# Score masks moved into the free contraction rows of a two-layer attention kernel, and one output turn per unit instead of two

## Chip, cores and metric

One core of one Trainium2 chip. The metric is the device time of one launch in microseconds, the median of several executions. TensorE is PE in the profile (its weight loads PEld), VectorE DVE, ScalarE ACT, GpSimd POOL, SyncE SP.

## What is computed

Two transformer layers on x of 4 x 1024 x 128, in float32 precision. The parts that the change touches are the two masked attentions of 16 heads of 8:

```
# layer 0, xn = layernorm(x)
scores = einsum('bhqd,bhkd->bhqk', q / sqrt(8), k)
scores = where(pos_q >= pos_k, scores, -inf)
out    = einsum('bhqk,bhkd->bhqd', softmax(scores), v) @ Wout.T
x = x + out + fp4_ffn(xn)                 # blockwise FP4 feed-forward

# layer 1, xn = layernorm(x); keys: the first token, then a convolution of stride 3 (342 keys)
mask   = (3 * k_idx >= q_idx + 0.001)
scores = einsum('bhqd,bhkd->bhqk', q, k) * 8 ** -0.5 + mask * -1e9
o      = einsum('bhqk,bhkd->bhqd', softmax(scores), v) @ Wo.T + bo
x = x + o + moe_ffn(xn)                   # 8 experts, top 2, and a shared one
```

## The kernel before, in words

The program is six stages, one block each with a barrier between them: first_projection, quantised_ffn, attention of layer 0, between_layers, attention of layer 1, experts.

**Attention.** A unit is one batch and a group of four heads (16 units a layer). Each q and k is kept as three bf16 parts, whose products stand as 96 contraction rows (KROWS) in qp (96 + 3 rows, 4 heads, 1024 queries) and kp (two pairs of heads); rows 96 to 98 carry minus the row maximum in qp and ones in kp. Four group buffers of each rotate (GROUPS = 4). A unit goes through these steps, each an entry of a list that Geometry.order (L758) writes beforehand from planned costs, and that every engine follows:

- "fill" (PE L1041, DVE L1154): scores of a tile of 128 queries by its keys go to one of three PSUM banks, and DVE's TENSOR_REDUCE takes the row maximum. A bank holds one, two or four heads, by the width (128 to 512 columns in layer 0, with a separate leading fill of 512 for the upper query tiles; 43 to 342 in layer 1). A fill on the diagonal begins with a matmul of the identity with mask_s (L1051), which writes -1e30 or -1e9 into the last 128 (layer 0) or 43 to 44 (layer 1) columns of each head; the fills proper then add onto it (L1054).
- "tail" and "turn_max": DVE splits the maxima in three bf16 parts, PE turns them, DVE copies them out, SP stores them into rows 96 to 98 of qp (L956).
- "pair" (L1075): scores again, keys on partitions, 99 rows, for two heads; ACT takes the exponential (L1136), POOL zeroes the unseen part (L992).
- "weigh" (L1091): vh (values of 8 columns, a column of ones, in a field of VW = 32) by the exponentials, four heads beside each other, onto p_o. The steps of the first 512 queries (c = 0) come before those of the second (c = 1); each half has its own start and stop in p_o.
- "end" and "turn_out": after each half ACT copies p_o to o_raw (L1145), PE turns it in four transposes into one of the three banks (L1067), DVE takes the reciprocal of the sums (L1194) and multiplies (L1198). The next half's first weigh waits for the copy.
- "next_load": SP loads the operands of the unit four further on with twelve DMAs (load_operands).

**First projection.** DVE normalises, quantises and splits x chunk by chunk (8 chunks of 512 tokens, normalise L360, fp4_scales, fp4_round, fp4_rescale), then PE and ACT follow. POOL builds the constants at the start: squares (L293 to L298), the ones of kp (four memsets, L303), the masks (L308 to L326), vh and others, with root(b) (L282) between them, which gives DVE the 1/std of a batch; root(2) and root(3) stand at its end.

**Between the layers.** POOL does root(n) for each of 8 chunks and nothing else (L1294, L1296); DVE adds, takes the moments and normalises, PE and ACT project, and SP stores the parts of q and k (L190) and, from the fourth chunk on, loads the operands of the first groups of layer 1.

## Time and profile before

| | us |
|---|---|
| median of 3 runs | 1237.9 (1234.62 to 1257.37) |
| the profiled execution | 1236.83 |
| its span in the profile | 1234.9 |
| first projection and FP4 feed-forward | 0 to 188.7 |
| attention, layer 0 | 188.7 to 693.4 |
| between the layers | 693.4 to 775.9 |
| attention, layer 1 | 775.9 to 1001.0 |
| experts | 1001.0 to 1234.9 |

Times in the rows are microseconds from the start of the span, unless the row gives a mean in ns. In a group row come the operation, out<-in, shapes and count, then busy us and mean ns of one, then the idle time before it and who ended it. In a timeline row "x2" means two instructions merged, and the second figure is the length from the start of the first to the end of the last. PE's matmuls are pipelined and overlap in the rows.

### The profile page before, as it was taken

The page shows a single profiled execution, that of the slowest core. Times are in us where ns is not written, and L with a number is a line of the kernel's source. Part 1 is how long each engine was busy: PE and PEld are TensorE (multiplying, and loading weights), DVE is VectorE, ACT ScalarE, POOL GpSimd, SP SyncE. Part 2 cuts the span into 40 slices and gives each one's busy share as a digit, 9 for nine tenths or more (in the row PEclk, how much of TensorE's full clock was granted, in tenths as well). Part 3 has the DMA queues.
Part 4 walks back from the last instruction along what each step waited for, and adds up shares of the span by engine and source line. Part 5 has one row for each costly group of instructions (what it writes and reads, how often), then busy time and mean ns, then how long its engine had stood idle before and what let it go on. Part 6 is the DMA issues. An engine that isn't in the chain of part 4 may idle for free. (4 is left out here: it accounts for less than half of the span.)

```text
span 1234.9 us, 22211 instructions
## 1 busy us (share of the span) xinstructions
PE 1122.0 (91%) x7511; PEld 614.9 (50%) x7518; DVE 935.3 (76%) x2098; ACT 735.9 (60%) x1148; POOL 447.5 (36%) x714
## 2 busy tenths in 40 slices
PE   4668879999999999999998697799999989999997
PEld 2345663344444444343443374444444448888874
DVE  7979988688888888888884372877787636777776
ACT  3557640666666666666666453356666667787762
POOL 6002220142323332332222120387776622566630
PEclk9989996899999999999999897799999989999999
DMA  4322790003302130212000013222222253687542
GB/s 137 96 84 64 113 125 2 19 27 108 101 13 93 41 116 23 82 55 85 28 2 2 1 54 86 67 64 61 64 65 61 58 169 127 188 258 245 163 122 83
DMA packets 94975, 103.52 MB, mean 84 GB/s; under 512 B 17217, under 2 KB 72838, under 8 KB 94864
## 3 DMA queue, kind: packets, MB, share of 16 engines
q1 hardware_dynamic: 88928, 93.09, 28.0%
q0 software_dynamic: 4992, 8.48, 2.0%
q8 instruction: 61, 1.00, 0.3%
q10 hardware_dynamic: 944, 0.54, 0.2%
q14 instruction: 50, 0.41, 0.1%
HBM read 64.67 MB, written 38.43 MB: 83 GB/s over the span
## 5 line engine op out<-in xcount | busy, mean ns | idle before, releaser
L1136 ACT ACTIVATE a_probs<-a_pst 128x1024 f32<-128x1024 f32 (+4 forms) x544 | 413.9, 813 | 274.9 <-PE a_pst L1084 274.3
L1160 DVE TENSOR_REDUCE a_tops<-a_ps 128x1 f32<-128x512 f32 (+9 forms) x624 | 340.9, 589 | 84.4 <-PE a_ps L1054 76.6
L992 POOL TENSOR_SCALAR_AFFINE_SELECT a_probs<-a_probs 128x256 f32<-128x256 f32 (+3 forms) x384 | 180.6, 481 | 366.8 <-ACT a_probs L1136 361.4
L1054 PE MATMUL a_ps<-kp,qp 96*128 96x512 bf16 (+9 forms) x1280 | 293.5, 307 | 0.0
L1084 PE MATMUL a_pst<-qp,kp 99*128 99x512 bf16 (+4 forms) x1088 | 259.1, 330 | 15.2 <-DMA qp<-a_top_rows 11.5
L1103 PE MATMUL a_po<-a_probs,vh 128*32 128x512 f32 (+4 forms) x2176 | 232.0, 499 | 2.6 <-POOL a_probs L992 2.5
L1160 DVE TENSOR_REDUCE a_tops_lead<-a_ps 128x1 f32<-128x512 f32 x256 | 161.6, 681 | 5.9 <-PE a_ps L1054 5.6
L1054 PEld LDWEIGHTS a_ps<-kp,qp 96*128 96x128 bf16 x1280 | 111.4, 100 | 79.1 <-DVE a_tops_lead L1160 15.5
L1051 PE MATMUL a_ps<-mask_s,identb 128*128 128x128 bf16 (+8 forms) x624 | 144.1, 234 | 6.8 <-PEq L1254 4.4
L1084 PEld LDWEIGHTS a_pst<-qp,kp 99*128 99x128 bf16 (+1 forms) x1088 | 91.8, 99 | 110.9 <-ACT a_probs L1136 47.2
L1738 POOL DMA_INDIRECT chosen_rows<-e_slot_y,e_slot_x x92 | 93.3, 1014 | 97.0 <-DVE e_slot_y L1958 75.3
L1051 PEld LDWEIGHTS a_ps<-mask_s,identb 128*128 128x128 bf16 x624 | 59.2, 98 | 125.9 <-DVE a_tops L1160 66.8
L1946 DVE TENSOR_TENSOR e_tails<-e_hidden,e_heads 128x512 fp32r<-128x512 f32 x124 | 85.8, 692 | 40.2 <-ACT e_heads L1880 38.1
L1103 PEld LDWEIGHTS a_po<-a_probs,vh 128*32 128x32 f32 (+1 forms) x2176 | 43.4, 108 | 71.3 <-issue 60.9
L1873 ACT ACTIVATE e_hidden<-e_pup,e_slot_b 128x512 f32<-128x512 f32 x92 | 63.2, 687 | 25.7 <-PE e_pup L1751 23.6
L1004 POOL DMA_INDIRECT slot_rows<-rows,slots x64 | 63.7, 995 | 14.1 <-issue 12.0
L151 POOL TENSOR_TENSOR f_hq<-f_v,f_sc 128x704 f32<-128x704 f32 x16 | 22.7, 1422 | 119.2 <-DVE f_v L711 117.5
L1194 DVE RECIPROCAL a_inv_sum<-a_ps 128x16 f32<-128x16 f32 x64 | 16.3, 255 | 62.8 <-PE a_ps L1072 61.4
L1072 PE MATMUL a_ps<-ident,a_o_raw 128*128 128x128 f32 x256 | 41.8, 286 | 3.5 <-ACT a_o_raw L1145 1.9
L1145 ACT ACTIVATE a_o_raw<-a_po 128x512 f32<-128x512 f32 x64 | 38.4, 599 | 10.3 <-PE a_po L1103 10.3
L597 PE MATMUL f_pg<-wg,big 128*128 128x352 f32 x64 | 28.0, 522 | 16.2 <-DVE f_h L692 15.2
L1944 DVE CAST e_heads<-e_hidden 128x512 fp32r<-128x512 f32 x62 | 27.0, 435 | 18.7 <-ACT e_hidden L1873 18.1
(314 smaller groups left out, 1624.0 us busy)
## 6 DMA issues: line engine op xcount, KB each, us to landing
e_slot_w<-weight_parts SPq DMA_DIRECT2D x23, 1024.0 KB
qp<-q_parts SPq DMA_DIRECT2D x64, 96.0 KB
slot_rows<-empty_row SPq DMA_DIRECT2D x4, 1495.0 KB, 27.2
e_slot_x<-slot_rows SPq DMA_DIRECT2D x23, 260.0 KB, 3.1
a_raw<-in_wraw SPq DMA_DIRECT2D x18, 256.0 KB, 3.6
weight_parts<-first_rows SPq DMA_DIRECT2D x9, 512.0 KB, 3.0
weight_parts<-a_cut SPq DMA_DIRECT2D x9, 512.0 KB, 3.1
qp<-q_parts SPq DMA_DIRECT2D x64, 64.0 KB
```

Of the source, the lines that this page charges most:

```text
L992: pool.affine_select(out=seen, in_=seen, compare_op=ALU.is_ge, fill=0.0, base=m0, pattern=[[0, 2], [1, mw]], channel_multiplier=-1 if laye ...
L1004: pool.indirect_dma_start(dram["slots"], bass.IndirectOffsetOnAxis(sb["slots"][:, choice, t:t + 1], 0), sb["rows"][:, t, :], None, bounds_ ...
L1051: pe.matmul(out, sb["identb"][:, :], mask_s[r][:, 0:mw].unsqueeze(1).broadcast_to([P, nh, mw]), start=True, stop=False, skip_group_check=True)
L1054: last = pe.matmul(bank[:, i * room:i * room + w], sb["qp"][slot][0:KROWS, j, f["qt"] * P:(f["qt"] + 1) * P], sb["kp"][slot][0:KROWS, j // ...
L1072: last = pe.transpose(turned[:, t * P:(t + 1) * P], o_raw[:, t * P:(t + 1) * P], sb["ident"][:, :])
L1084: last = pe.matmul(p_st[half][0:st["rows"], i, off:CHUNK], sb["kp"][slot][0:KROWS + PARTS, half, st["kt"] * P:st["kt"] * P + st["rows"]], ...
L1103: last = pe.matmul(p_o[VW * j:VW * (j + 1), st["off"]:CHUNK], sb["vh"][n % 2][0:st["rows"], st["kt"], j, :], probs[local % RING][0:st["row ...
L1136: act.activation(probs[local % RING][0:st["rows"], 2 * part:2 * part + 2, st["off"]:CHUNK], p_st[part][0:st["rows"], :, st["off"]:CHUNK], ...
L1160: dve.tensor_reduce(out, scores, AX.X, ALU.max).then_inc(s["banks_read"], 1)
L1738: pool.indirect_dma_start(dram["chosen"], bass.IndirectOffsetOnAxis(slot_x[r % XR][:, t, E:E + 1].bitcast(U32), 0), slot_y[r % YR][:, t, : ...
L1873: act.activation(hidden[m % RR][:, :], p_up[m % UR][:, :], ACT.Gelu, bias=biases(j)[:, k:k + 1])\
L1946: dve.tensor_tensor(tails[m % HR][:, :], hidden[m % RR][:, :], heads[m % HR][:, :].bitcast(F32), ALU.subtract)\
```

## The change

- Masks: the identity matmul of each diagonal fill, mask_s0 and mask_s1 go. qp and kp get AFTER = 26 rows more (CROWS = 96 + 3 + 26 = 125). They hold powers of two such that their product is 0 for a seen key and hugely negative for an unseen one. Each head of a diagonal fill is written by two matmuls: the columns left of the mask with 96 rows, the masked columns with 125. Since rows 96 to 98 are then part of a fill, qp's maxima must be zero there: next_load gets one more DMA, which loads zeros from no_maxima.
- The rows are drawn by POOL: in the first projection at its end (draw_after: memsets, ten selects, and eight copies into kp and qp of the four groups), and between the layers after root(n) (draw_after twice for each of the first four chunks, lay_after for each of the last four).
- Sums: vh gets fields of VROW = 48 with the values at VAT = 16, and the first half reads the field from column 16, the second from column 0. So the sums of both halves stand in p_o beside each other (rows 0 to 8 and 16 to 24 of each 32), p_o is started once a unit, copied once and turned once. DVE takes one reciprocal of twice the elements, and two multiplications as before.
- wqkv, wg, wu and wd are given free after the feed-forward. The planner's costs follow.

```diff
 @block.gpsimd of first_projection
+            def draw_after():
+                row0 = KROWS + PARTS
+                pool.memset(after_k[:, :], 0.0).then_inc(drawn, 1)
+                pool.memset(after_q[:, :], -2.0 ** (EQUAL - KEY0 + JUMP)).then_inc(drawn, 1)
+                pool.wait_ge(drawn, 2)
+                pool.affine_select(out=after_q[:, :], in_=after_q[:, :], compare_op=ALU.is_ge, fill=0.0,
+                                   base=-STEP * row0 - 1, pattern=[[-1, P]], channel_multiplier=STEP).then_inc(drawn, 1)
+                pool.wait_ge(drawn, 3)
+                for d in range(STEP):
+                    pool.affine_select(out=after_k[:, :], in_=after_k[:, :], compare_op=ALU.not_equal,
+                                       fill=2.0 ** (KEY0 + JUMP * d), base=STEP * row0 - d, pattern=[[1, P]],
+                                       channel_multiplier=-STEP).then_inc(drawn, 1)
+                    pool.affine_select(out=after_q[:, :], in_=after_q[:, :], compare_op=ALU.not_equal,
+                                       fill=-2.0 ** (EQUAL - KEY0 - JUMP * d) if d < STEP - 1 else 0.0,
+                                       base=STEP * row0 - d, pattern=[[1, P]], channel_multiplier=-STEP).then_inc(drawn, 1)
+                    pool.wait_ge(drawn, 3 + 2 * (d + 1))
+                done = 3 + 2 * STEP
+                pool.memset(after_k[KROWS:KROWS + PARTS, :], 1.0).then_inc(drawn, 1)
+                pool.wait_ge(drawn, done + 1)
+                for g in range(GROUPS):
+                    for rows, after in ((sb["kp"][g], after_k), (sb["qp"][g], after_q)):
+                        wide = rows[KROWS:CROWS, :, :].rearrange("r j (t n) -> r (j t) n", n=P)
+                        pool.tensor_copy(wide, after[KROWS:CROWS, :].unsqueeze(1).broadcast_to(list(wide.shape)))\
+                            .then_inc(drawn, 1)
...
-            for g in range(GROUPS):
-
-                pool.memset(sb["kp"][g][KROWS:KROWS + PARTS, :, :], 1.0).then_inc(built, 1)
-                pool.wait_ge(built, 5 + g + 1)
-                if g >= GROUPS // 2 - 1 and g < GROUPS // 2 + 1:
-                    root(g - (GROUPS // 2 - 1))
-                    pool.wait_ge(root_steps, 2 * (g - (GROUPS // 2 - 1)) + 2)
-            pool.memset(sb["mask_s0"][:, :], 0.0).then_inc(built, 1)
-            pool.memset(sb["mask_s1"][:, :, :], 0.0).then_inc(built, 1)
+            for b in range(2):
+                root(b)
+                pool.wait_ge(root_steps, 2 * b + 2)
...
             for b in (2, 3):
                 root(b)
+            draw_after()
 attention, SP
                 if what == "next_load":
...
+                    sp.dma_start(sb["qp"][n % GROUPS][KROWS:KROWS + PARTS, :, :].rearrange("r j t -> r (j t)").bitcast(F32),
+                                 dram["no_maxima"]).then_inc(sb["loaded"][n % GROUPS], 16)
 attention, PE
-                if f["mask"]:
-
-                    r, mw = f["mask"]
-                    out = bank[:, :].rearrange("p (h k) -> p h k", h=nh)[:, :, w - mw:w]
-                    pe.matmul(out, sb["identb"][:, :], mask_s[r][:, 0:mw].unsqueeze(1).broadcast_to([P, nh, mw]),
-                              start=True, stop=False, skip_group_check=True)
+                plain = w - f["mask"][1] if f["mask"] else w
                 for i, j in enumerate(f["heads"]):
...
+                    for rows, at, to in ((KROWS, 0, plain), (CROWS, plain, w)):
+                        if at < to:
+                            last = pe.matmul(bank[:, i * room + at:i * room + to],
+                                             sb["qp"][slot][0:rows, j, f["qt"] * P:(f["qt"] + 1) * P],
+                                             sb["kp"][slot][0:rows, j // 2, f["k0"] + at:f["k0"] + to],
+                                             start=True, stop=True, skip_group_check=True)
...
-                    last = pe.matmul(p_o[VW * j:VW * (j + 1), st["off"]:CHUNK], sb["vh"][n % 2][0:st["rows"], st["kt"], j, :],
+                    last = pe.matmul(p_o[VW * j:VW * (j + 1), st["off"]:CHUNK], sb["vh"][n % 2][0:st["rows"], st["kt"], j, v0:v0 + VW],
                                      probs[local % RING][0:st["rows"], j, st["off"]:CHUNK],
-                                     start=st["first"], stop=st["last"], tile_position=(0, VW * j),
+                                     start=k == 0, stop=k == S - 1, tile_position=(0, VW * j),
 attention, DVE
-                dve.reciprocal(inv_sum[:, :, :], turned[:, :, :, D]).then_inc(s["inverse_done"], 1)
+                dve.reciprocal(inv_sum[:, :, :, :], turned[:, :, :, D:D + VAT + 1:VAT]).then_inc(s["inverse_done"], 1)
 @block.gpsimd of between_layers (root(n) is the old body)
+            def lay_after(g):
+
+                for rows, after in ((sb["kp"][g][KROWS:CROWS, :, 0:KEYS1], after_k), (sb["qp"][g][KROWS:CROWS, :, :], after_q)):
+                    pool.tensor_copy(rows, after[KROWS:CROWS, :].unsqueeze(1).broadcast_to(list(rows.shape)))\
+                        .then_inc(drawn, 1)
...
+                root(n)
+                if n < CHUNKS // 2:
+                    draw_after(2 * n)
+                    draw_after(2 * n + 1)
+                if n >= CHUNKS // 2:
+                    pool.wait_ge(s["root_steps"], START + 2 * n + 2)
...
+                if n >= CHUNKS // 2:
+                    lay_after(n - CHUNKS // 2)
```

Here draw_after(t) is one memset, five pairs of selects with a wait after each pair, and a last select, on 42 to 44 columns of after_k and 128 of after_q.

## Rows read from the trace of the kernel before

**Rows 1.** windows of the two attention stages; figures in us, instructions in brackets
```profile
core 0: us, PE busy (x) PEld busy (x) DVE busy (x) ACT busy (x) POOL busy (x), PEclk, DMA share, GB/s
188.70:693.40 504.70, 493.16 (x3568) 195.67 (x3569) 402.95 (x768) 304.66 (x417) 140.71 (x308) 0.97 0.15 49
775.90:1001.00 225.10, 210.77 (x1888) 101.58 (x1888) 162.11 (x418) 136.34 (x193) 158.42 (x236) 0.96 0.24 62
```

**Rows 2.** windows: steady parts of both attentions, end of the projection
```profile
300.00:552.00 252.00, 250.89 (x1895) 102.30 (x1894) 213.87 (x408) 158.62 (x220) 82.44 (x174) 1.00 0.21 65
820.00:970.00 150.00, 142.78 (x1333) 69.99 (x1331) 115.03 (x300) 96.75 (x137) 113.43 (x168) 1.00 0.25 63
40.70:78.70 38.00, 24.29 (x112) 14.69 (x112) 35.81 (x70) 24.24 (x49) 0.03 (x1) 0.91 0.33 104
```

**Rows 3.** timeline of PE, layer 0 (start us, us, engine, line, operation)
```profile
304.11 0.38 PE L1051 MATMUL a_ps<-mask_s,identb 128*128 128x512 bf16 x1
304.33 0.39 PE L1054 MATMUL a_ps<-kp,qp 96*128 96x128 bf16 x4
...
308.86 0.22 PE L1051 MATMUL a_ps<-mask_s,identb 128*128 128x128 bf16 x1
308.92 0.38 PE L1054 MATMUL a_ps<-kp,qp 96*128 96x512 bf16 x1
...
314.31 0.63 PE L1072 MATMUL a_ps<-ident,a_o_raw 128*128 128x128 f32 x4
314.78 0.28 PE L1084 MATMUL a_pst<-qp,kp 99*128 99x128 bf16 x2
```

**Rows 4.** timeline of SP's queue, layer 0: stores of the maxima
```profile
214.21 0.80 SPq L956 DMA_DIRECT2D qp<-a_top_rows  x1
...
632.44 32.02 SPq L956 DMA_DIRECT2D qp<-a_top_rows  x2
```

**Rows 5.** timeline of PE, layer 1
```profile
911.56 0.18 PE L1051 MATMUL a_ps<-mask_s,identb 128*128 128x43 bf16 x1
911.59 0.29 PE L1054 MATMUL a_ps<-kp,qp 96*128 96x299 bf16 x1
```

**Rows 6.** costliest groups of the page: one reciprocal per turn
```profile
L1194 DVE RECIPROCAL a_inv_sum<-a_ps 128x16 f32<-128x16 f32 x64 | 16.3, 255 | 62.8 <-PE a_ps L1072 61.4
```

**Rows 7.** groups of POOL by shape, and a select of its timeline
```profile
L975 POOL COPY vh<-rows 128x256 f32<-128x256 f32 x16 | 6.3, 396 | 8.3 <-POOLq L531 6.1 <-PE a_po L1103 2.2
L975 POOL COPY vh<-v 128x64 f32<-128x64 f32 x16 | 4.0, 251 | 34.7 <-POOLq L1254 34.7
...
2.12 0.28 POOL L298 TENSOR_SCALAR_AFFINE_SELECT minus_identb<-minus_identb 128x128 bf16<-128x128 bf16 x1
```

**Rows 8.** timelines of POOL and DVE, where they meet and where not
```profile
14.04 1.80 POOL L303 MEMSET kp<- 3x2048 bf16 x1
...
14.57 1.31 DVE L125 TENSOR_SCALAR n_sc<-n_am 128x32 f32<-128x32 f32 x1
...
74.10 0.18 DVE L125 TENSOR_SCALAR n_sc<-n_am 128x32 f32<-128x32 f32 x1
...
176.62 0.89 DVE L711 SCALAR_TENSOR_TENSOR f_v<-f_v,f_m 128x704 f32<-128x704 f32 x1
...
177.59 1.97 POOL L151 TENSOR_TENSOR f_hq<-f_v,f_sc 128x704 f32<-128x704 f32 x1 [4.51 <-DVE f_v L711]
...
178.35 1.95 DVE L711 SCALAR_TENSOR_TENSOR f_v<-f_v,f_m 128x704 f32<-128x704 f32 x1
```

**Rows 9.** timelines of POOL, SP and ACT between the layers
```profile
699.80 0.20 POOL L1294 TENSOR_SCALAR b_var<-b_var 128x4 f32<-128x4 f32 x1 [9.69 <-DVE b_var L164]
704.65 0.19 POOL L1294 TENSOR_SCALAR b_var<-b_var 128x4 f32<-128x4 f32 x1 [3.56 <-DVE b_var L164]
...
744.00 1.80 SPq L190 DMA_DIRECT2D k_parts<-k_kept  x3
...
754.78 0.60 ACT L1450 ACTIVATE q_kept<-b_pq 128x512 bf16<-128x512 f32 x1 [7.91 <-DMA q_parts<-q_kept]
```

More of the change, by code:

```diff
@@ L49 @@
 KROWS = 2 * PROWS
+STEP = 5
+AFTER = -(-P // STEP)
+SET = -(-(P // 3 + 2) // STEP)
+CROWS = KROWS + PARTS + AFTER
+JUMP, EQUAL, KEY0 = 25, -2, -50
 VW = 32
+VAT = 16
+VROW = VAT + VW
 EPS = 1e-5
-LOW0 = -1e30
-LOW1 = -1e9
 EXPONENT = 0x7F800000
@@ L94 @@
 ROW = E + 2
+NONE = 64
 NOWHERE = 1 << 24
@@ L760, in order @@
         S, F, units = self.S, self.F, B * GROUPS
-        fill_pe = [len(f["heads"]) * max(LOAD_US, f["width"] * COLUMN_US) + len(f["heads"]) * f["mask"][1] * COLUMN_US
-                   if f["mask"] else max(LOAD_US, f["width"] * COLUMN_US) for f in self.fills]
+        fill_pe = [len(f["heads"]) * f["width"] * COLUMN_US for f in self.fills]
         fill_dve = [REDUCE_US + len(f["heads"]) * f["width"] * LANE_US for f in self.fills]
@@ L852, in counted_before @@
     units = B * GROUPS
-    ends = T // CHUNK * units
     uses = sum(what in BANK_USES for what, *_ in geo.order())
@@ L856, in counted_before @@
                   exp_done=2 * units * geo.S, unseen_zeroed=2 * units * len(geo.masked), pv_done=units * geo.S,
-                  v_staged=units, o_copied=ends, inverse_done=ends)
+                  v_staged=units, o_copied=units, inverse_done=units)
     return {name: START + layer * count for name, count in layer0.items()}
@@ L876, in attention @@
     v_all = sb[f"v{layer}"]
-    mask_s = [sb["mask_s0"][:, :]] if layer == 0 else [sb["mask_s1"][:, r, :] for r in range(STRIDE)]
     with ExitStack() as ctx:
@@ L980, in stage @@
                     rows = geo.keys - full * P
-                    last = pool.tensor_copy(dst[0:rows, full, :, 0:D],
+                    last = pool.tensor_copy(dst[0:rows, full, :, VAT:VAT + D],
                                             v_all[0:rows, v0 + full, f0:f0 + GH * D]
@@ L1138, in _ @@
                         .then_inc(s["exp_done"], 1)
-                if what == "end":
-                    act.wait_ge(s["pv_done"], since["pv_done"] + S * n + 1 + max(
-                        i for i, st in enumerate(geo.steps) if st["c"] == k))
+                if what == "end" and k == T // CHUNK - 1:
+                    act.wait_ge(s["pv_done"], since["pv_done"] + S * (n + 1))
                     if last_out is not None:
@@ L1291, in _, with root @@
         def _(pool):
-            for n in range(CHUNKS):
+            def root(n):
                 pool.wait_ge(s["moment_steps"], START + 6 * (n + 1))
@@ L1297, in _, with draw_after @@
                     .then_inc(s["root_steps"], 1)
+            DRAWS = 2 * STEP + 2
+            def draw_after(t):
+                row0, rest, base = KROWS + PARTS + t % 2 * SET, P * t % STRIDE, 1 + DRAWS * t
+                first, last = P * t // STRIDE, (P * t + P - 1) // STRIDE + 1
+                ks, qs = after_k[:, first:last], after_q[:, t * P:(t + 1) * P]
+                pool.memset(qs, -2.0 ** (EQUAL - KEY0 + JUMP)).then_inc(drawn, 1)
+                for d in range(STEP):
+                    pool.wait_ge(drawn, base + 1 + 2 * d)
+                    pool.affine_select(out=ks, in_=ks, compare_op=ALU.not_equal, fill=2.0 ** (KEY0 + JUMP * d),
+                                       base=STEP * row0 - d, pattern=[[1, last - first]], channel_multiplier=-STEP)\
+                        .then_inc(drawn, 1)
+                    pool.affine_select(out=qs, in_=qs, compare_op=ALU.is_ge,
+                                       fill=-2.0 ** (EQUAL - KEY0 - JUMP * d) if d < STEP - 1 else 0.0,
+                                       base=STRIDE * (d - STEP * row0) - rest - 1, pattern=[[-1, P]],
+                                       channel_multiplier=STRIDE * STEP).then_inc(drawn, 1)
+                pool.wait_ge(drawn, base + 1 + 2 * STEP)
+                pool.affine_select(out=qs, in_=qs, compare_op=ALU.is_ge, fill=0.0, base=row0 + SET - 1, pattern=[[0, P]],
+                                   channel_multiplier=-1).then_inc(drawn, 1)
```

98 lines of the change are left out of this document (54 added, 44 removed).

## The prediction

> **What bounds the kernel now.** I read the busy time by stage first. In both attention stages TensorE is busy for nearly the whole stage (493.16 of 504.70 us in layer 0, 210.77 of 225.10 us in layer 1), while VectorE has 402.95 and 162.11 us [rows 1]. In the steady part of layer 0 this sharpens: PE 250.89 of 252.00 us, DVE 213.87, ACT 158.62; in layer 1 PE 142.78 of 150.00, DVE 115.03, POOL 113.43 [rows 2]. A busy PE counts the tails of pipelined matmuls, so I read its timeline next for the distance from start to start, which is what a matmul costs: the mask matmul of 128 columns starts at 308.86 and the fill behind it at 308.92, so a mask costs 0.06 us though it "takes" 0.22; the mask of 512 columns (304.11) holds PE 0.22 us until 304.33; four transposes (314.31) hold it 0.47 us until 314.78 [rows 3]. Cost goes with columns, and the weight load of each hides under the matmul before it. The unit is then read from SP's stores of the maxima: the first at 214.21, the last of layer 0 about 664.0 (the second of the pair that ends at 664.46), 15 units later: 30.0 us a unit [rows 4]. Layer 1 has 225.10 / 16 = 14.1 us a unit [rows 1]. The third stage to look at is the first projection: from 40.7 to 78.7 us DVE is busy 35.81 of 38.00 us, and POOL 0.03 [rows 2]: DVE alone sets its end. So three places matter: PE in the attentions, DVE in the projection, and the chain DVE, POOL, DVE between the layers.
>
> **The change, part by part.** *Masks, layer 0.* A unit has 22 fills with a mask: two of 512 mask columns, four of 256, sixteen of 128; 4096 columns in all. At 0.22, 0.11 (half of the 0.22) and 0.06 us that is 0.44 + 0.44 + 0.96 = 1.84 us [rows 3]. Against it, 24 fills are cut in two (all but the four narrowest and the four leading ones of each upper query tile); the columns stay the same, and a further matmul adds what 0.22 for 512 columns and 0.06 for 128 leave beyond proportion, about 0.005 us: 0.1 us. More rows in the contraction cost nothing by the rows: columns set the time. Net 1.7 us a unit on PE.
>
> *Masks, layer 1.* 17 masks a unit: three of about 173 columns, six of about 87, eight of 43 or 44. The narrow one costs 0.03 us (911.56 to 911.59) [rows 5]; the others by columns 0.08 and 0.04: 0.24 + 0.24 + 0.24 = 0.7 us. But 28 of 32 fills are cut, and the second part has 43 or 44 columns, for which a separate matmul costs 0.03 where its share of a wide one costs 0.02: +0.3 us. Net 0.4 us.
>
> *One turn per unit.* One of two sets of four transposes goes: 0.47 us of PE [rows 3]. DVE loses one reciprocal of 0.26 us (the one that stays has twice the elements, which I price at nothing: bounds 0 and 0.26) [rows 6], ACT one copy of p_o, and the second half no longer waits for it. So PE is relieved of 1.7 + 0.5 = 2.2 us a unit in layer 0 and 0.9 in layer 1. DVE stands at 213.87 / 252 of 30.0 = 25.5 us a unit and comes to 25.2; PE after would be at 27.8. DVE is then busy 91% instead of 85%, three banks stand between the two, and some of what PE saves it will wait for a bank. I take 80%: 1.8 us x 15 units = 27 us. Bounds: 15 x 0.3 (DVE keeps its idle time, below) and 15 x 2.2 = 33. In layer 1 PE also waits for the tail of the maxima, which doesn't shrink: I take two thirds, 0.6 x 16 = 10 us, with bounds 3 and 15. The fills of unit 0 in both layers are paced by DVE and gain nothing.
>
> *Drawing the rows in the first projection.* This is what the change pays. The POOL memsets of kp and the mask selects go from the start; behind the last root (POOL's work ends at 40.7) come 14 small operations and eight copies: four of 2048 and four of 4096 elements a partition. A POOL copy of 256 elements has 396 ns, one of 64 has 251 [rows 7]; the two give a fixed part of 0.2 us and 0.76 ns an element, the POOL memset of 2048 elements in 1.80 us [rows 8] gives 0.88. With 0.2 us and 0.82 ns a copy has 1.9 or 3.6 us, and all eight 22 us (bounds 20, and 29 at 0.4 us and 1.06 ns, a third above the middle). POOL is free until the next stage, so the copies themselves end in time. What they do to DVE: at 14.57 a DVE TENSOR_SCALAR of 32 elements took 1.31 us instead of 0.18 (74.10) and ended when the POOL memset of 14.04 did; at 178.35 a SCALAR_TENSOR_TENSOR took 1.95 us instead of 0.89 (176.62) and had to wait for POOL's f_hq [rows 8]. The loser of the two waits for the whole of the other's instruction. Copies follow one another without a wait between them, so between two of them DVE gets about one operation of 0.2 to 0.7 us through. Then eight copies take 22 + 8 x 0.5 = 26 us, in which DVE does some 6 us of its work: it loses 20 us, and the stage with it, since DVE has no slack there. Bounds: 0 (no copy stands in these rows) and 26. The small operations I price at +1, and what the memsets at the start cost DVE (1.13 us in the row of 14.57) at -1: nothing together.
>
> The Trainium skill, "SBUF — State Buffer", section "Who interferes with whom", speaks against this part: DVE instructions in a 2-port mode or with two SBUF inputs contend with a GpSimd instruction that reads SBUF, and the loser blocks for the whole of it, while one-input operations outside that mode pass. By this rule the reductions and reciprocals of a chunk would run beside the copies, and the loss would be 19 to 20 us; were the copies free, it would be none. The trace agrees in the two collisions named above.
>
> *Drawing between the layers.* POOL's root of a chunk stands in the chain: it starts at 699.80, the next at 704.65, 4.85 us a chunk [rows 9]. Behind each of the first four come two draws of 12 small operations. A select has 0.28 us [rows 7]; with half of the waits beside them I take 0.27 us each, 3.2 us a draw, 6.4 a chunk; with the root itself (0.2 + 0.1 + 1.0) POOL needs 7.7 us a chunk. Three chunks are late by 2.9 us, the fourth (7.0 us before) by 0.7: +9.5. From the fifth on POOL copies 684 + 4096 elements, 4.4 us, which fits into the chunk of some 6 us, but the moments on DVE collide with it: +0.5 in all up to the place that matters. That place is SP's store of k of the second batch (744.00): from there its queue of stores and loads holds ACT (754.78, 7.91 us of waiting for the store) until the stage ends [rows 9]. So the stage ends 10 us later. Bounds: 3 (small operations at 0.14 us) and 17 (0.36 us each, and copies that block).
>
> *At nothing:* the load of zeros over the maxima rows (one DMA of 24 KB more behind the twelve of a unit; they are issued more than two units ahead; if that cover is gone, 1 us a unit), the wider vh, the wait for the 4 + 1 later loads at the start of layer 0 (SP has nothing to issue there before 214.21).
>
> Sum: -27 - 10 + 20 + 10 = -7 us. The profiled execution took 1236.8 us, 1.1 under the median of 1237.9; -7 gives 1230 for it and 1231 for the median.
>
> **Rivals.** *The copies hardly block DVE* (the small partition count, or DVE wins the port each time): projection +2, between +4; 1237.9 - 27 - 10 + 6 = 1207. For it: no copy is seen against DVE in this trace. Against it: both collision rows. *DVE becomes the pace of layer 0, slower than before:* the reductions wait for fills 4.5 us a unit now; if that idle time is one of latency and stays, a unit takes 25.2 + 4.5 = 29.7 us, the gain is 0.3 x 15 = 4 instead of 27, and with the 30 us of POOL's drawing: 1237.9 - 4 - 10 + 30 = 1254. It decides as soon as a unit shrinks by less than 1.3 us (then 15 units don't pay for 30 - 10 us). For it: 85% busy with three banks. Against it: PE's stream is dense in the timeline, and DVE's waits end with PE's fills. *The change doesn't do what it says:* the second part of each cut fill shows its weight load (0.1 us) instead of hiding it: 24 x 0.1 and 28 x 0.07 us a unit eat the whole gain of both layers, 1237.9 + 30 + 5 = 1273. Against it: a mask with its own load costs 0.03 us in layer 1 [rows 5].
>
> **How the numbers follow.** Forecast 0.54, free copies 0.27, DVE's pace 0.15, visible loads 0.04. The range 1204 to 1257 takes in the first three with their bounds. A measurement of this kernel tells about 2% (25 us) from no change: under 1213 lies most of the second case and a little of the first, 0.27; over 1263 the last and the far end of the third, 0.07; the rest 0.66.
>
> **What would show it.** Right: no matmul of mask_s; the stage of layer 0 shorter by some 27 us and a unit at 28.2 us; 32 turns instead of 64; in the projection DVE operations of 2 to 4 us beside POOL copies of 3.6 us, and the next stage 20 us later; roots of the first chunks between the layers 7.7 us apart. Wrong: DVE operations at their old length beside the copies (then 1207), or layer 0 within 10 us of before with DVE waiting as long as now (then 1254).

## The result, and the profile after

The changed kernel takes 1314.4 us (median of 4 runs, 1312.15 to 1316.76) against 1238.0 us: a ratio of 1.062, 95% interval 1.059 to 1.065. I had forecast 1231, no change. Of the four runs of the kernel before, the one at 1257.4 us was in a slower state and stands in no ratio. The profiled execution has a span of 1312.7 us, 77.8 more than before. By stage, each from its first instruction to the first of the next (so layer 1 holds here the gap ahead of the experts, too):

| stage, us | before | after | measured | forecast |
|---|---|---|---|---|
| first projection | 80.3 | 98.9 | +18.6 | +20 |
| feed-forward | 108.4 | 109.2 | +0.8 | 0 |
| attention, layer 0 | 504.7 | 516.7 | +12.0 | -27 |
| between the layers | 82.6 | 100.1 | +17.5 | +10 |
| attention, layer 1 | 227.9 | 256.2 | +28.3 | -10 |
| experts | 231.1 | 231.6 | +0.5 | 0 |

The windows of the two attentions and the stage between them, after (start:end, length, then the busy us of PE, PEld, DVE, ACT and POOL, the granted clock as a share of full speed, DMA share, GB/s):

```profile
208.10:724.80 516.70, 476.48 (x3536) 186.69 (x3536) 401.38 (x752) 301.49 (x401) 142.21 (x308) 0.94 0.15 48
724.80:825.00 100.20, 70.07 (x320) 50.96 (x325) 56.27 (x267) 32.66 (x74) 50.58 (x123) 0.74 0.17 46
825.00:1078.50 253.50, 210.25 (x2000) 101.42 (x1999) 171.97 (x401) 132.34 (x177) 157.90 (x236) 0.90 0.21 57
```

Against [rows 1] PE's busy time in layer 0 did fall, from 493.16 to 476.48 us, and DVE's is what it was (401.38 against 402.95): the matmuls are gone, yet the stage is longer. PE now idles 40 us where it idled 11.5. In layer 1 the granted clock fell from 0.96 to 0.90. So PE waits for something new. Two of its waits in layer 0, after (who waited <- for whom: us in total, times, longest), and then the first of them before:

```profile
PE a_pst L1106 <- DMA qp<-a_top_rows: 17.0, 16, 1.3
PE a_ps L1076 <- DVE o L1220: 4.4, 7, 0.6
```

```profile
PE a_pst L1084 <- DMA qp<-a_top_rows: 4.0, 8, 1.7
```

The wait that grew is that of a unit's first pair for its row maxima, on their way from DVE over PE's turn, DVE's copy and SP's store into qp. The place in the timeline of PE, after:

```profile
417.42 0.85 PE L1076 MATMUL a_ps<-kp,qp 125*128 125x128 bf16 x12
418.20 1.08 PE L1125 MATMUL a_po<-a_probs,vh 128*32 128x256 f32 x16
419.21 0.26 PE L1085 MATMUL a_ps<-identb,a_top_parts 128*96 128x128 bf16 x1
419.65 0.34 PE L1076 MATMUL a_ps<-kp,qp 96*128 96x256 bf16 x2 [0.18 <-DVE a_tops L1181]
420.34 0.63 PE L1094 MATMUL a_ps<-ident,a_o_raw 128*128 128x128 f32 x4 [0.34 <-DVE a_top_rows L1208]
420.80 0.50 PE L1076 MATMUL a_ps<-kp,qp 96*128 96x256 bf16 x4
421.94 0.34 PE L1076 MATMUL a_ps<-kp,qp 96*128 96x256 bf16 x2 [0.64 <-DVE o L1220]
423.53 0.60 PE L1106 MATMUL a_pst<-qp,kp 99*128 99x512 bf16 x2 [1.25 <-DMA qp<-a_top_rows]
```

Read it from the turn of the maxima at 419.21 to the first pair that needs them at 423.53. In between the order has only a turn of the sums (420.34) and a few fills, all for the same three banks, and DVE must empty each: it holds the copy of the maxima, a reciprocal, two multiplications and reductions. PE waits at nearly every step. The first line answers a rival, too: twelve matmuls with 125 rows span 0.85 us, of which the last one's tail is 0.22, so they start 0.057 us apart, as the 128 columns of [rows 3] did (0.06). Neither the rows nor a weight load show.

What follows these waits stands in two windows of the same kernel:

```profile
421.00:424.10 3.10, 1.22 (x9) 0.50 (x8) 2.24 (x6) 0.00 (x0) 0.00 (x0) 1.00 0.21 68
424.10:427.50 3.40, 3.40 (x15) 1.75 (x13) 2.21 (x4) 2.64 (x3) 0.81 (x2) 0.50 0.26 78
```

PE works 1.22 of 3.10 us, and for the next 3.4 us its granted clock is 0.50, the 1.2 GHz level. That comes back at every second unit (362.7, 424.1, 485.6, 547.0, 608.4, 669.9 us, each 3.4 us long, and 6.8 us at 297.8): 27 us at half clock, by my estimate (one half of it) about 14 us of work lost. Before, there is none of these between 224 and 691 us ([rows 2] has 1.00).

In layer 1 a second place is worse. SP's queue and PE, after:

```profile
872.98 0.43 SPq L986 DMA_DIRECT2D qp<-no_maxima  x1
873.47 0.78 SPq L207 DMA_DIRECT2D qp<-q_parts  x1
...
882.53 0.44 SPq L986 DMA_DIRECT2D qp<-no_maxima  x1
883.02 0.76 SPq L979 DMA_DIRECT2D qp<-a_top_rows  x1
```

```profile
880.69 0.61 PE L1076 MATMUL a_ps<-kp,qp 96*128 96x170 bf16 x8
886.17 1.03 PE L1106 MATMUL a_pst<-qp,kp 99*128 99x512 bf16 x2 [4.88 <-DMA qp<-a_top_rows]
```

A next_load is thirteen issues of some 0.7 us on SP. Here the order has two of them in a row, and the store of the maxima (883.02) stands behind the second. DVE had the maxima ready 6.0 us earlier (and 4.9 us at one later unit); before, each of the 32 stores starts within 0.1 us of DVE's copy. From the turn of the maxima of each of those two units to the next it is 22.2 and 19.6 us instead of 13.2.

The two late stores are 10.9 us. Just as large is the wait of the weighs for POOL, which zeroes the unseen part of the exponentials. Layer 1, after, then before:

```profile
PE a_po L1125 <- POOL a_probs L1017: 12.0, 10, 1.8
```

```profile
PE a_po L1103 <- POOL a_probs L992: 1.2, 1, 1.2
```

POOL is as busy in both (157.90 against 158.42 us). In both_kept, a kernel of the next section that has the same instructions in the old order, this wait is 1.6 us: it comes with the order.

The two stages with drawing read as forecast in kind. POOL in the projection, after, and DVE's groups there (mean ns of one); last the same three operations before:

```profile
46.10 1.89 POOL L322 COPY kp<-n_after_k 29x2048 bf16<-29x2048 bf16 x1
47.94 3.60 POOL L322 COPY qp<-n_after_q 29x4096 bf16<-29x4096 bf16 x1
```

```profile
L152 DVE TENSOR_TENSOR n_v<-n_v,n_m 128x512 f32<-128x512 f32 x3 | 5.4, 1785 | 0.1
L148 DVE TENSOR_SCALAR n_m<-n_m 128x512 f32<-128x512 f32 x3 | 4.6, 1520 | 0.1
L127 DVE TENSOR_REDUCE n_am<-n_xn 128x32 f32<-128x512 f32 x3 | 2.0, 680 | 0.0
```

```profile
L146 DVE TENSOR_TENSOR n_v<-n_v,n_m 128x512 f32<-128x512 f32 x5 | 3.5, 691 | 0.2
L121 DVE TENSOR_REDUCE n_am<-n_xn 128x32 f32<-128x512 f32 x5 | 3.4, 677 | 0.0
L142 DVE TENSOR_SCALAR n_m<-n_m 128x512 f32<-128x512 f32 x5 | 2.1, 427 | 0.2
```

A subtraction or a scaling takes 1.5 to 1.8 us beside the copies instead of 0.4 to 0.7; a reduction, with one input, takes what it took. By the Trainium skill, "SBUF — State Buffer", section "Who interferes with whom", only the port pair that the two engines share contends, and the reduction does not use it; the trace agrees (680 against 677 ns).

POOL between the layers, after:

```profile
731.52 1.03 POOL L1321 TENSOR_TENSOR rstd<-b_var,minus_half 128x4 f32<-128x4 f32 x1
...
740.17 1.03 POOL L1321 TENSOR_TENSOR rstd<-b_var,minus_half 128x4 f32<-128x4 f32 x1
...
748.83 1.01 POOL L1321 TENSOR_TENSOR rstd<-b_var,minus_half 128x4 f32<-128x4 f32 x1
...
768.54 3.60 POOL L1348 COPY qp<-b_after_q 29x4096 bf16<-29x4096 bf16 x1
```

The roots are 8.7 us apart, where 4.85 was the distance before [rows 9] and 7.7 the forecast.

### The profile page after: what moved, and what is told of

It is laid out like the page before. It is cut to its first block and busy times, and to the rows that moved or that the text cites. A ratio compares the mean times of both kernels' runs of the same rounds, so it can differ in the third digit from the quotient of the medians.

```text
span 1312.7 us, 22404 instructions
## 1 busy us (share of the span) xinstructions
PE 1117.5 (85%) x7591; PEld 614.2 (47%) x7598; DVE 979.4 (75%) x2066; ACT 728.4 (55%) x1116; POOL 510.2 (39%) x832
## 5 line engine op out<-in xcount | busy, mean ns | idle before, releaser
L1076 PE MATMUL a_ps<-kp,qp 96*128 96x256 bf16 (+10 forms) x2112 | 297.7, 258 | 15.5 <-DVE a_tops L1181 4.7
L1106 PE MATMUL a_pst<-qp,kp 99*128 99x512 bf16 (+4 forms) x1088 | 271.7, 345 | 42.3 <-DMA qp<-a_top_rows 29.7
L1076 PEld LDWEIGHTS a_ps<-kp,qp 96*128 96x128 bf16 (+1 forms) x2112 | 145.3, 101 | 228.7 <-DVE a_tops L1181 85.8
L1181 DVE TENSOR_REDUCE a_tops_lead<-a_ps 128x1 f32<-128x512 f32 x256 | 165.0, 685 | 23.7 <-PE a_ps L1076 23.1
L1106 PEld LDWEIGHTS a_pst<-qp,kp 99*128 99x128 bf16 (+1 forms) x1088 | 85.9, 102 | 136.4 <-ACT a_probs L1158 60.0
L1942 ACT ACTIVATE e_hidden<-e_pup,e_slot_b 128x512 f32<-128x512 f32 x92 | 62.6, 687 | 19.6 <-PE e_pup L1820 15.4
L1215 DVE RECIPROCAL a_inv_sum<-a_ps 128x32 f32<-128x32 f32 x32 | 11.4, 358 | 64.1 <-PE a_ps L1094 63.4
L1166 ACT ACTIVATE a_o_raw<-a_po 128x512 f32<-128x512 f32 x32 | 19.1, 597 | 68.9 <-PE a_po L1125 68.9
L1949 ACT ACTIVATE e_heads<-e_hidden 128x512 fp32r<-128x512 f32 x62 | 39.2, 632 | 2.0
L1820 PE MATMUL e_pdn<-e_tails,e_slot_w 128*128 128x512 f32 x92 | 36.0, 391 | 0.0
L1818 PE MATMUL e_pdn<-e_heads,e_slot_w 128*128 128x512 f32 x92 | 35.9, 390 | 0.0
```

What stands on the lines that cost most here:

```text
L1076: last = pe.matmul(bank[:, i * room + at:i * room + to], sb["qp"][slot][0:rows, j, f["qt"] * P:(f["qt"] + 1) * P], sb["kp"][slot][0:rows, ...
L1106: last = pe.matmul(p_st[half][0:st["rows"], i, off:CHUNK], sb["kp"][slot][0:KROWS + PARTS, half, st["kt"] * P:st["kt"] * P + st["rows"]], ...
L1181: dve.tensor_reduce(out, scores, AX.X, ALU.max).then_inc(s["banks_read"], 1)
L1818: pe.matmul(out_, w_h, m_head, start=start, stop=False, skip_group_check=True)
L1820: return pe.matmul(out_, w_h, m_tail, start=False, stop=stop, skip_group_check=True)
L1942: act.activation(hidden[m % RR][:, :], p_up[m % UR][:, :], ACT.Gelu, bias=biases(j)[:, k:k + 1])\
```

## The experiments

My theory after this reading: **the order is at fault.** Geometry.order plans every step from costs, and with one turn a unit and without the mask matmuls it writes another list. A letter each (F fill, P pair, W weigh, t tail, M turn of the maxima, O turn of the sums, L next_load, e end), from a tail on, as both planners write them:

```
layer 0, before   tPPWPPFMLLFWFFFWFFPFPF       layer 1, before   tPPOWMLPWePFFOFFPFPFFW
layer 0, after    tPPWPPFFFWWeMLLFOFFFPF       layer 1, after    tPWeWPPFFMLFWFFFWeFFPO
```

The lines of layer 0 are every second unit; in the others M is followed by two pairs of the unit before, in both lists. In the units shown the two weighs that stood between M and the next pair, PE's longest steps, now stand ahead of M. In layer 1 M itself comes later, and twice early in the list there is an LL that the old list doesn't have. The rivals: the new instructions cost more than priced (instruction theory), or holding p_o over a whole unit stalls PE (turn theory). The first four kernels separate order, masks and turn.

**both_kept.** The changed kernel in the old order:

```diff
+    def planned_before(self):
...
     def order(self):
+        return [(what, n, 0 if what == "turn_out" else k, part) for what, n, k, part in self.planned_before()
+                if what != "turn_out" or k == T // CHUNK - 1]
```

> The changed kernel, with the planner's order of before (its list, less the turn of each first half) in both attentions. Order theory: the changed kernel loses in the attentions because its planner, fed with new costs, writes an order in which PE waits more; with the old order the layer-0 stage goes from 516.7 us to about 482 (504.7 of before less the 1.7 + 0.5 us a unit of PE work removed, at most 15 units), layer 1 from 253.5 to about 218, the whole from 1314 to about 1245. Instruction theory: the cut fills or the 125 rows cost more than their columns; then the order changes nothing and the stages stay near 515 and 250. Turn theory: holding p_o over the whole unit is what stalls PE; then they stay long here and in turn_kept, but not in masks_kept.

Measured: 1280.6 us, ratio 1.037 (1.034 to 1.039); layer 0 492.5, layer 1 238.4. Against the changed kernel the order alone costs 24.2 and 17.8 us in the profiled executions. That of both_kept was the fastest of its five (1271.8 us, the median is 1280.6), and by the medians the order costs 33.8 us in all; the two kernels further down that keep this order have 491.4 and 489.1 us in layer 0, but 252.7 and 246.3 in layer 1. So the cost in layer 0 is firm (24 to 28 us), and in layer 1 it is something between 4 and 18. And the rest falls short of the theory: 12 us gained in layer 0 instead of 22, and 10 or more lost in layer 1.

What the order costs in layer 0 is not the wait that I had followed. PE waits 17.0 us for the stored maxima in the changed kernel and 14.1 in both_kept (its line is shown below). Of the 24.2 us, 13.2 are PE's busy time (476.48 against 463.30 us for the same 3536 matmuls), about what the stretches at half clock cost by the estimate above, and 11.0 its idle time: 3 more for the maxima and, by the largest groups of waits, some 6 more for DVE and 3 for ACT and POOL.

**masks_kept.** The hunks of the masks alone; the turn's hunks (vh, p_o, turn_out, scale_out) and the planner as before:

```diff
-                if f["mask"]:
-                    pe.matmul(out, sb["identb"][:, :], mask_s[r][:, 0:mw].unsqueeze(1).broadcast_to([P, nh, mw]), ...
+                    for rows, at, to in ((KROWS, 0, plain), (CROWS, plain, w)):
```

> Masks as contraction rows alone: two turns a unit, and exactly the order of before. Order theory: layer 0 about 504.7 - 15 x 1.4 = 484 us, layer 1 about 219, projection and between-layer stages as in the changed kernel (98.9 and 100 us): about 1237.9 + 19 + 18 - 21 - 6 = 1248. Instruction theory: layer 0 at or above 505, layer 1 above 225, the whole 1275 or more.

Measured: 1270.2 us, ratio 1.028 (1.026 to 1.031); layer 0 499.1, layer 1 230.5. 5.6 us gained where 21 were expected, by neither theory.

**turn_kept** and **turn_own.** The hunks of the turn alone, first in the old order less the turns of the first halves, then in the planner's own:

```diff
-                    if st["first"]:
-                        pe.wait_ge(s["o_copied"], since["o_copied"] + 2 * n + st["c"])
+                    pe.wait_ge(s["o_copied"], since["o_copied"] + n)
```

> One turn a unit alone, the masks by matmul as before, and the order of before less the turns of the first halves. PE loses 0.47 us of transposes and one bank use a unit. Order theory: layer 0 about 498 us (16 x 0.4 less), layer 1 about 220, the whole about 1227. Turn theory (p_o held over the unit makes PE wait): layer 0 above 505 and layer 1 above 230.

> The same kernel as turn_kept in its work, but in the order that the planner writes itself for one turn a unit, with its fill costs of before. Order theory: whatever this order differs in shows against turn_kept: if an order with one turn is worse by itself, layer 1 has 235 us or more and the whole is 10 to 25 us above turn_kept. Instruction and turn theories: no difference above 3 us from turn_kept, since the instructions are the same.

Measured: turn_kept 1233.5 us, ratio 0.999 (0.997 to 1.001); layer 0 496.0, layer 1 228.2. turn_own 1258.2 us, ratio 1.017 (1.014 to 1.020); 510.1 and 244.3. The same instructions in another order are 25 us apart. The turn theory falls: with p_o held over the unit, layer 0 is 8.7 us shorter than before (in an execution that was the fastest of ten, 4 us under their median; the whole kernel is no faster than before). So does the instruction theory as an explanation of the loss. Since turn_own plans with the fill costs of before, it isn't these costs either: one turn instead of two is enough to tip the list.

Where the masks' gain went is in the waits for the maxima in layer 0, masks_kept, then both_kept:

```profile
PE a_pst L1106 <- DMA qp<-a_top_rows: 13.7, 15, 2.0
```

```profile
PE a_pst L1112 <- DMA qp<-a_top_rows: 14.1, 15, 2.0
```

The old order leaves just enough work between M and the pair to cover the store. Take PE's work out of that stretch and the store sticks out: 13.7 us against 4.0, 9.7 of the missing 15. How long it is shows at SP and PE of both_kept:

```profile
822.56 0.76 SPq L985 DMA_DIRECT2D qp<-a_top_rows  x1
```

```profile
825.77 0.83 PE L1112 MATMUL a_pst<-qp,kp 99*128 99x512 bf16 x2 [1.16 <-DMA qp<-a_top_rows]
```

3.2 us from issue to use; the planner counts 2.2 (STORE_US). Over all pairs that waited, the median is 2.8 us before and in turn_kept, and 3.2 in masks_kept and both_kept. So a part of the 9.7 us, by my estimate up to 15 x 0.4 = 6, is no lost cover but a use that itself comes later in the kernels with mask rows. The store doesn't move slower there: its 96 packets run from 1.4 to 1.9 us after the issue in before and masks_kept alike, and what makes PE start 0.4 us later behind them no run here shows.

I had seen the 3.2 us alone, and the theory became sharper: **an order is good when it covers 3.2 us behind each turn of the maxima**, and the next kernels plan with 3.3. At the same time the two drawing stages were taken apart.

**moved_draws** and **all_by_dma.** both_kept, with these edits:

```diff
 first projection, POOL
-                        pool.tensor_copy(wide, after[KROWS:CROWS, :].unsqueeze(1).broadcast_to(list(wide.shape)))
 feed-forward, SP
+                    sp.dma_start(wide, after[KROWS:CROWS, :].unsqueeze(1).broadcast_to(list(wide.shape)))
 feed-forward, POOL, behind each of the first eight fp4_rescale; gone between the layers
+                    draw_after(i)
 all_by_dma only, between the layers, SP at its start instead of lay_after on POOL
+                    sp.dma_start(rows, after[KROWS:CROWS, :].unsqueeze(1).broadcast_to(list(rows.shape)))
```

> both_kept with two edits in two stages. (1) The eight POOL copies at the end of the first projection go; SP lays the rows by eight DMAs in the feed-forward stage instead. Port theory (POOL's copies block VectorE): projection back from 99.5 to 80 to 82 us. Rival: something else in the longer POOL list delayed it (the later roots, the selects); then it stays above 90. (2) The 96 small drawing operations leave POOL's queue between the layers for POOL's idle time in the feed-forward stage; the eight copies of the rows (0.75 and 3.6 us) stay between the layers. Queue theory (the roots stood behind the draws): the stage between goes from 100.5 to about 86 us; if the copies are what costs, it stays above 93. The feed-forward stage may pay 0 to 8 us. The whole: about 1280 - 18 - 14 = 1248.

> moved_draws, and the rows of layer 1 also laid by eight DMAs that SP issues at the start of the stage between. If the POOL copies beside the second half of the chunks block VectorE as in the projection, the stage loses another 3 to 5 us against moved_draws and comes to 82.5 to 84; if they stand in free time, no difference. The whole about 1245. With all drawing costs gone, what is left over 1237 is the cost of the two changes in the attentions themselves: layer 0 -12, layer 1 +10.

Measured: 1308.2 us, ratio 1.057 (1.053 to 1.061), and 1327.7, ratio 1.077 (1.071 to 1.082). The two stages of moved_draws answer as expected: the projection is back at 79.9 us (port theory: POOL's copies block DVE), and the stage between at 85.1 (queue theory: the roots stood behind the draws; the copies cost 2.5 us of the 17.5). The first five of POOL's roots stand 4.84 us apart again:

```profile
753.68 1.01 POOL L1357 TENSOR_TENSOR rstd<-b_var,minus_half 128x4 f32<-128x4 f32 x1
...
758.52 1.01 POOL L1357 TENSOR_TENSOR rstd<-b_var,minus_half 128x4 f32<-128x4 f32 x1
```

The later three, with the copies between them, are still 9.0 to 10.0 us apart, and the stage hardly feels it.

What I had not expected is the price of the DMAs, which made the feed-forward stage 171 us long (with the draws and without the DMAs it has 118, as laid_by_act will show). SP, moved_draws:

```profile
87.19 0.75 SPq L591 DMA_DIRECT2D kp<-after_k  x1
87.98 6.98 SPq L591 DMA_DIRECT2D qp<-after_q  x1
95.01 15.19 SPq L591 DMA_DIRECT2D kp<-after_k  x1
110.23 7.75 SPq L591 DMA_DIRECT2D qp<-after_q  x1
```

A DMA that writes 29 rows in pieces of 128 bf16 holds SP for 7 to 15 us as soon as one stands before it, and the loads of the operands wait behind. In all_by_dma the same at the start of the stage between made that 104.0 us.

Both kernels keep the order of both_kept and yet differ from it in layer 1 (252.7 and 246.3 us against 238.4). PE does the same 2000 matmuls and idles as long in all three (33.8, 33.0 and 33.1 us); what differs is its busy time, 218.8, 213.3 and 205.3 us at a mean granted clock of 0.85, 0.87 and 0.92. Two units of all_by_dma in one order, from one turn of the maxima to the next, show it in small:

```profile
958.30:974.60 16.30, 14.53 (x129) 6.71 (x126) 9.98 (x25) 8.26 (x12) 10.53 (x16) 0.79 0.21 53
1003.50:1016.60 13.10, 11.71 (x129) 5.67 (x125) 10.21 (x27) 8.05 (x12) 9.27 (x15) 1.00 0.26 67
```

129 matmuls each; at 0.79 granted clock the unit takes 16.3 us, at 1.00 13.1. PE waits 1.8 us for the maxima in the first and 1.4 in the second; over the stage, waits of 1.1 to 2.2 us went with the slow clock and others of 1.2 to 1.7 did not. By the Trainium skill, "TensorE: Matmul & The Clock Gate", section "HAM oscillation — how this bites in real kernels", a wait for a transfer that comes back at every tile can bring the slow clock back at every tile. Here it came back at some units and not at others; what decides between them no run here shows.

**turn_tuned** and **both_tuned.** The planner's numbers, the order left to itself:

```diff
-AHEAD = (0.35, 0.6)
+AHEAD = (0.35, 0.45)
     def order(self):
+        PASS_US, COLUMN_US, STORE_US = ((0.07, 0.00042, 3.3), (0.25, 0.00045, 3.3))[self.layer]
```

> One turn a unit, masks by matmul, and the planner writes the order itself, but with the latency of the maxima that the traces show (from SP's store to PE's first pair 3.2 us, planned with 2.2; now 3.3), and in layer 1 0.25 instead of 0.07 us from engine to engine and a lead of 0.45 instead of 0.6 units. Latency theory (what the orders differ in is how much of the wait for the maxima they cover): layer 0 about 491 us instead of 510 (turn_own) or 496 (turn_kept), layer 1 about 217 instead of 244 or 228, the whole about 1217. Rival: VectorE or the banks set the pace and the order is only luck: layer 0 within 3 us of 496 to 510, layer 1 above 228.

> Masks as rows (drawn and laid as in all_by_dma), one turn a unit, fill costs of before in the planner, and its other costs as in turn_tuned. Latency theory: layer 0 about 487 us, layer 1 about 217, projection and between as in all_by_dma, the whole about 1212: faster than before by 2%. Rival (the rows cost PE or DVE what the mask matmuls cost): no faster than turn_tuned, layer 0 at 491 or above.

Measured: turn_tuned 1230.4 us, ratio 0.995 (0.993 to 0.997); layer 0 495.7, layer 1 228.5. So against its own planner it gains 14 and 16 us, and against the old order nothing: the expectation of 491 and 217 was too high. both_tuned 1299.0 us, ratio 1.052 (1.049 to 1.054), slower than before for the DMAs' price in two stages as in all_by_dma; layer 0 481.0, layer 1 229.4. Layer 0 is 15 us under turn_tuned: with the store covered, the masks are worth what they weren't in masks_kept.

How far does the cover go as the cause? In layer 0 turn_own and turn_tuned differ in one number alone, STORE_US (2.2 and 3.3), and the stage falls by 14.4 us; but PE's wait for the maxima was 6.5 us in turn_own and is gone in turn_tuned, so less than half of it is this wait, and the rest comes with the new list and was not traced. In layer 1 the theory doesn't hold. PE's waits for the maxima there, turn_kept, then turn_own:

```profile
PE a_pst L1090 <- DMA qp<-a_top_rows: 18.2, 16, 1.4
```

```profile
PE a_pst L1085 <- DMA qp<-a_top_rows: 3.8, 3, 2.5
```

The kernel with the long wait takes 228.2 us and the one with the short wait 244.3. Three of the planner's numbers changed together in layer 1, and no run tells them apart: that these lists are better is shown, why is not.

**before_tuned, masks_tuned, laid_by_act.** The other corners under the same planner. In the last two ScalarE lays layer 0's rows while it clears qp:

```diff
-                act.activation(sb["qp"][g][0:KROWS, 2 * half:2 * half + 2, :], ..., ACT.Copy, scale=0.0)
+                wide = sb["qp"][g][0:CROWS, 2 * half:2 * half + 2, :].rearrange("r j (t n) -> r (j t) n", n=P)
+                act.activation(wide, sb["after0"][1][0:CROWS, :].unsqueeze(1).broadcast_to(list(wide.shape)), ACT.Copy)
+                wide = sb["kp"][g][KROWS:CROWS, half:half + 1, :].rearrange("r j (t n) -> r (j t) n", n=P)
+                act.activation(wide, sb["after0"][0][KROWS:CROWS, :].unsqueeze(1).broadcast_to(list(wide.shape)), ACT.Copy)
```

> The kernel before with the planner's numbers of turn_tuned and nothing else. It is the fourth corner beside turn_tuned (495.7 and 228.5 us in the attentions), masks_tuned and laid_by_act under the same planner. If the masks' matmuls and the second turn cost what the trace of before says, layer 0 is at about 495.7 + 6 = 502 us here, layer 1 at 225 to 230, the whole 1230 to 1240.

> Masks as rows, two turns a unit, the same planner numbers. The rows are drawn as in moved_draws (in the feed-forward stage, the rows of layer 1 laid by POOL between the layers) and those of layer 0 are laid by ScalarE in the instructions that clear qp. Masks are worth 1.4 us a unit where the maxima are covered: layer 0 at 483 to 487 us. If they are worth only the 0.4 us a unit of masks_kept, 497. Layer 1 within 3 us of 228.

> both_tuned with cheap laying: the eight clearing instructions of ScalarE in the feed-forward stage copy 125 rows of the drawn pattern instead of 96 rows of zeros (same elements a partition), eight more ScalarE copies of 1024 elements fill the rows of kp (about 1.1 us each by the 1.9 us for 2048), the draws of layer 1 stand in POOL's idle time there, and POOL's copies of layer 1 stay between the layers. Projection 80, feed-forward 109 to 115, layer 0 481, between 85, layer 1 229, experts 231: about 1217 to 1222, 1.3% under before. If ScalarE's eight copies pace the feed-forward stage, it is 118 and the whole 1226.

Measured: before_tuned 1235.6 us, ratio 1.000 (0.998 to 1.001); masks_tuned 1236.1, ratio 1.001 (0.999 to 1.002); laid_by_act 1226.3, ratio 0.992 (0.990 to 0.994). The attentions, in us:

| planner numbers of turn_tuned | layer 0 | layer 1 |
|---|---|---|
| before_tuned: mask matmuls, two turns | 501.2 | 230.8 |
| turn_tuned: mask matmuls, one turn | 495.7 | 228.5 |
| masks_tuned: masks as rows, two turns | 490.7 | 229.5 |
| laid_by_act: both | 482.0 | 228.4 |

In layer 0 the turn is worth 5.5 us, the masks 10.5, both 19.2. masks_tuned missed its 483 to 487 by 4 us. In layer 1 the four are 1 to 2 us apart, in one profiled execution each: too little to tell from nothing. The waits for the maxima in layer 0 of laid_by_act:

```profile
PE a_pst L1134 <- DMA qp<-a_top_rows: 2.5, 7, 0.5
```

2.5 us in all, against 17.0 (after), 14.1 (both_kept) and 13.7 (masks_kept). The feed-forward stage is still 118.1 us instead of 108.4. DVE's operation in it that grew most, laid_by_act:

```profile
L131 DVE TENSOR_SCALAR f_sc<-f_am 128x44 f32<-128x44 f32 x16 | 9.5, 592 | 0.6
```

**draws_in_attention.** One small drawing operation behind each of POOL's selects in layer 0:

```diff
 attention, POOL
                 if what == "pair" and geo.steps[k]["mask"]:
                     zero_unseen(n, k, part)
+                    next(draws, None)
```

> laid_by_act, with the 97 drawing operations of layer 1 moved from the feed-forward stage into attention layer 0, one behind each of POOL's selects there. Port theory: in the feed-forward stage POOL's draws block VectorE's small operations (the scale's TENSOR_SCALAR takes 592 ns on average there instead of 185, 6.5 us over 16), so that stage returns from 118.1 to 110 to 112 us and that operation to about 185 ns, and layer 0, where VectorE is idle a fifth of the time, pays less than 4 us: the whole about 1220. Rival: the eight copies of kp's rows on ScalarE (8.4 us) are what paces the feed-forward stage; then it stays at 117 or above, and the whole at 1226 to 1230.

Measured: 1218.9 us, ratio 0.987 (0.985 to 0.989); feed-forward 110.0, layer 0 480.4. The operation, draws_in_attention:

```profile
L131 DVE TENSOR_SCALAR f_sc<-f_am 128x44 f32<-128x44 f32 x16 | 3.5, 220 | 0.6
```

The draws were the cost and ScalarE's copies are not: 8.1 us of stage for 6.0 us of this one operation, and 110.0 us is also what turn_kept has, which lays nothing. In layer 0, where DVE is idle a fifth of the time, they cost nothing that shows. This is the best of all kernels here, 1.3% under the one before: its interval ends below 1, but it is less than the 2% that the prediction took as the least change to be told.

## Why the prediction was wrong

- **The failed step is "1.8 us x 15 units = 27 us", and with it "0.6 x 16 = 10 us".** It takes PE's relief as shorter units in an order that stays as it is. My own front page says that the planner's costs follow, and I gave that no price and no rival. PE's busy time in layer 0 did fall by 29.9 us in the old order (493.16 to 463.30; 33 was the bound), so the relief was priced right and the path was wrong. The new order costs 24.2 us in layer 0 and 17.8 in layer 1 (changed kernel against both_kept, one execution each): 42 of the 77.8 us, or 34 by the medians. How it costs them is only in part known: half clock behind many small waits in layer 0, late stores and waits for POOL in layer 1.
- **The share of the relief that arrives was too high as well.** In the old order it is 12.2 us of 33 in layer 0, and -10.5 or worse in layer 1, because the store of the maxima loses its cover and is used later by up to 0.4 us (waits of 14.1 us against 4.0, and 24.2 against 7.5). Where the order covers the store it is 19.2 us (before_tuned against laid_by_act). "In layer 1 PE also waits for the tail of the maxima, which doesn't shrink" named the right wait, and I let it take only a third of the gain. In the old order it took all of it.
- **The price on PE of the parts was right.** 125 rows cost no more than 96, a cut fill no more than its columns, no weight load shows; that rival (0.04) is out.
- **The rival at 1254 came nearest in layer 0, and its reason was half right.** It gave 29.7 us a unit; measured are 30.8, first store of the maxima to last, where before has 30.0. DVE is busy 401 of 517 us and is not the pace; but PE does wait for it longer than before, and for the store, and then runs at half clock.
- **The projection was right**: +18.6 for +20. The eight copies take 23.8 us (22 forecast), and moved_draws, without them, is back at 79.9 us. The free-copies rival (0.27) is out.
- **The stage between was right in kind and too small:** +17.5 for +10. A draw takes 3.7 us and not 3.2, so a chunk 8.7 instead of 7.7; and the later chunks, which I had taken as hardly touched, are 8.7 to 10 us apart where they were 5.9 to 7: POOL copies for 4.35 us behind each of their roots. Counted from the start of the stage, the fifth root is 13 us late (41.5 against 28.2) and the eighth 22 (69.2 against 46.9). moved_draws, without the draws, is 15.4 us shorter there than both_kept; its eighth root is still 8 us late (55.1 us against 46.9) and its stage only 2.5 us longer, so what the stage feels is the draws ahead of the fifth root, and the lateness behind it almost not.
- **"At nothing"** held for the wider vh. The DMA of zeros can't be told apart: it is one of the thirteen issues that made SP late, it takes 0.5 us of SP each time, so about 1 of the 6.0 us (an estimate), and before's twelve, twice in a row, would have made it late too. No kernel with mask rows ran without it.

In short, by the profiled executions: 18.6 + 17.5 from drawing, 42 from the order, and the masks and the turn themselves gave 12.2 and took 10.5 back; by the medians 8 of the 42 are rather the masks' and the turn's in layer 1. Undone or planned around one after the other, these lead to 1218.9 us.

## What to carry to other kernels

Where a planner writes the order of the work, a change of the work is a change of the order: compare the two lists before pricing anything, and look for what stands between a transfer's start and its first use. A saving on the bounding engine shortens the cover of a fixed latency beside it; price it by what becomes late next, and give the planner the latency that the trace shows (2.8 to 3.2 us here, not 2.2), though here that explained a part of what it brought and in layer 1 nothing. Before a stage's difference between two kernels is read from one execution each, see how far that execution is from its kernel's median: here that was 9 of 42 us. In this kernel constants drawn or copied by POOL were paid by DVE: put them where DVE has slack, or let an engine that already passes over the same rows lay them.

## What the runs showed of the hardware

- PE at full clock, busy 1.22 of 3.10 us, was followed by 3.4 us at 1.2 GHz. In all_by_dma a unit of the same 129 matmuls took 16.3 us at a mean granted clock of 0.79 and 13.1 at 1.00.
- The 24 KB store of the maxima from SBUF to SBUF moved its packets 1.4 to 1.9 us after the issue on SP, and PE's first use of it came at 2.8 us (before, turn_kept) or 3.2 us (masks_kept, both_kept), medians; the reason for the difference is open.
- Beside POOL's bf16 copies a subtraction of 128x512 f32 on DVE took 1785 ns on average instead of 691, a reduction of the same size 680 instead of 677.
- A DMA from SBUF to SBUF in pieces of 256 bytes held SP's queue for 7 us (928 pieces, behind one of 464) and 15 us (464 pieces, behind one of 928), where a load of the operands holds it for 0.7.
- ScalarE copied a pattern onto 125 partitions (1905 ns for 2048 elements) in the time that it took to clear 96 (1896 ns).
